# A second cross attention rebuilt as a stream of seven stages, with row turns, router logits and routing inside it

## The reference

```
x += tanh(g_xattn[0]) * cross_attention_0(layernorm(x), ctx)      # 16 heads of 64
x += tanh(g_ffn[0])   * six layers of (local attention, ffn)(layernorm(x))
x += tanh(g_xattn[1]) * cross_attention_1(ctx, layernorm(x))      # this change
x += tanh(g_ffn[1])   * mixture_of_experts(layernorm(x))          # and its router
```

```
attn  = softmax(q k^T / sqrt(8))                 # keys, values from ctx; 64 x 64 per head
gate  = 0.5 * mean_n(ctx @ w_la) + 0.5 * max_n(ctx @ w_la)        # one number per head
attn2 = softmax(gate * attn)
out   = (w * attn2 + (1 - w) * attn) @ v @ w_proj + b_proj
```

## Time and profile before

| | us |
|---|---|
| median of 3 runs (4242.39 to 4248.78) | 4245.28 |
| the profiled execution | 4245.7 |
| its span, first to last instruction | 4243.9 |

### The profile page before, as it was taken

How to read it: one execution, slowest core, us unless ns; L and a number is a source line. 1 busy time by engine, 2 the same in 40 slices (tenths; PEclk the granted TensorE clock), 3 DMA queues, 4 the chain that set the end, 5 groups by cost and what they waited for, 6 DMA issues and landing times.

```text
span 4243.9 us, 147344 instructions
## 1 busy us (share of the span) xinstructions
PE 4020.4 (95%) x50345; PEld 2806.3 (66%) x50345; DVE 3504.6 (83%) x7236; ACT 2999.4 (71%) x6796; POOL 2867.3 (68%) x3647
## 2 busy tenths in 40 slices
PE   5999998999999999999999999999999998788799
PEld 3777775666666666666666666666666666566665
DVE  4666667999888998899988998899989998677566
ACT  2555556888888888788878887888888887554322
POOL 2333337888888888888887888788888887555200
PEclk9999999999999999999999999999999999887699
DMA  3000001000000001000000001000010000000000
GB/s 89 6 7 7 6 4 48 10 8 10 24 22 9 9 8 34 12 8 9 24 21 8 10 7 31 16 10 7 10 35 11 7 10 9 18 12 11 2 10 10
DMA packets 162227, 64.81 MB, mean 15 GB/s; under 512 B 121556, under 2 KB 156128, under 8 KB 162016
## 3 DMA queue, kind: packets, MB, share of 16 engines
q1 hardware_dynamic: 162016, 62.05, 5.8%
HBM read 26.54 MB, written 2.10 MB: 7 GB/s over the span
## 4 chain that ended last, share of the span: by engine, by line
POOL 43%; issue 25%; PE 24%; DVE 5%; POOLq 2%; SPq 1%; ACT 1%; DVEq 0%; DMA 0%; ACTq 0%
POOL qn L646 10%; POOL qn L635 8%; POOL big L646 7%; POOL e L641 5%; POOL big L635 4%; PE pj L1506 3%; PE pp L1464 2%; PE po L1479 2%; PE sc L1861 2%; PE pj L1498 2%; PE pj L1547 1%; POOL rstd L657 1%; PE po L1485 1%; POOLq L389 1%; PE turn L1450 1%
## 5 line engine op out<-in xcount | busy, mean ns | idle before, releaser
L1573 PE MATMUL pj<-wqkv,xcT 128*128 128x512 f32 x1536 | 799.5, 602 | 17.0 <-issue 9.2
L646 POOL TENSOR_TENSOR qn<-qn,big 128x512 f32<-128x512 f32 x384 | 490.5, 1278 | 289.9 <-DVE big L1139 289.9
L818 ACT ACTIVATE big<-pj 128x512 f32<-128x512 f32 x768 | 473.7, 617 | 69.0 <-PE pj L1573 59.2
L1139 DVE TENSOR_TENSOR big<-pj,ropes 128x512 f32<-128x512 f32 x768 | 521.3, 679 | 0.0
L1145 DVE TENSOR_REDUCE ss<-big 128x8 f32<-128x512 f32 x768 | 514.8, 671 | 0.1
L646 POOL TENSOR_TENSOR big<-big 128x512 f32<-128x512 f32 x384 | 485.1, 1273 | 4.7 <-DVE big L1139 4.7
L1726 PEld LDWEIGHTS pp<-wo,oT 128*128 128x128 f32 x3072 | 358.7, 192 | 161.7 <-issue 82.6
L641 POOL TENSOR_TENSOR e<-e,rc 128x512 f32<-128x512 f32 x384 | 400.2, 1042 | 55.7 <-DVE rc L1169 55.7
L635 POOL TENSOR_TENSOR qn<-qn,ny 128x512 f32<-128x512 f32 x384 | 396.7, 1043 | 7.5
L635 POOL TENSOR_TENSOR big<-big,ny 128x512 f32<-128x512 f32 x384 | 396.2, 1043 | 7.6
L1726 PE MATMUL pp<-wo,oT 128*128 128x128 f32 x3072 | 395.4, 282 | 2.3 <-ACT oT L841 1.2
(11 more groups left out here) (320 smaller groups left out, 9938.3 us busy)
## 6 DMA issues: line engine op xcount, KB each, us to landing
wqkv<-in_L_ffn_Wqkv SPq DMA_DIRECT2D x18, 512.0 KB, 3.7
xsd<-Y SPq DMA_DIRECT2D x192, 32.0 KB
xsd<-Y SPq DMA_DIRECT2D x384, 15.8 KB
xsf<-Y SPq DMA_DIRECT2D x96, 64.0 KB
xsf<-Y SPq DMA_DIRECT2D x192, 31.5 KB
xsx<-Y SPq DMA_DIRECT2D x64, 64.0 KB, 1.8
xsx<-CT SPq DMA_DIRECT2D x64, 64.0 KB, 1.9
wo<-in_L_ffn_Wo SPq DMA_DIRECT2D x6, 512.0 KB, 4.2
```

Of the source, the lines that this page charges most:

```text
L646: nc.gpsimd.tensor_tensor(U[a.par][i], U[a.par][i], t2b[i % 2], ALU.add).then_inc(sem("d_add"), 1)
L818: nc.scalar.activation(sqb[i % 2], pj[i % 2][:, :], ACT.Square).then_inc(sem("d_sq"), 1)
L1139: nc.vector.tensor_tensor(t2v, swapped, sin, ALU.mult).then_inc(sem("d_r"), 1)
L1573: mm(pj[i % 2][:, :], xcT[:, a.par, :], wqkv[:, i * 512:i * 512 + 512], start=True, stop=True).then_inc(sem("d_ch"), 1)
```

## The change

The stream gets seven stages, called p[0] to p[6], and each body becomes a list of small functions called in a new order. Work is the same but for what follows.

- **Stages**: the row turn is a step of its own ahead of the projections. The second softmax and its turn share stage p[3], the first softmax with its values is in p[2]. p[6] is a tile whose residual was done two steps earlier.
- **Banks**: the row turn goes to pj[0], where the projections follow it. Turned probabilities of the first softmax go to pt_, of the second to pp (the other way round before). The gates go to columns of po[0], beside the value products, instead of pj[1]. The router's logits lie there too, and turned rows in po[1].
- **Scores** are done in two halves at two places: scores(p1, 0) late in one step, scores(p2, 1) first in the next.
- **Row turns and logits inside**: values2 also turns a normalised row tile, ACT copies it to CT (in the loop also to tmp, where PE reads it), and values1 multiplies it with the router weights. Normalised rows go to two small buffers r_in, not to Y. Tiles 30 and 31 are turned after the stream, and tiles 28 to 31 get their logits there.
- **DVE** loses two small instructions per tile (L1302 and L1330): a scalar_tensor_tensor takes the constant with it.
- **Routing** for tiles 0 to 27 is put behind DVE's steps 34, 35 and 36 (7, 8 and 4 instructions, with an exponential on ACT). That of tiles 28 to 31 (19 small instructions) lies ahead of and between the first group's experts.
- **Experts**: the first group is written out, the other seven are the loop. PE issues up of the first expert right behind the last residual, ahead of the last row turns.

The core of the diff (conditions on missing tiles, and functions whose instruction is unchanged, are cut):

```diff
-        r_turn = [pt_, pp, pj[0], pj[1]]
-        r_logits = po[0][:, 0:NT * NE].rearrange("p (t x) -> p t x", x=NE)
+        l_gates, r_logits = po[0][:, 144:144 + L1H], po[0][:, 160:160 + NT * NE].rearrange("p (t x) -> p t x", x=NE)
+        r_rows = po[1][:, 144:144 + 2 * P]
+        r_in = [xsd[:, i, :] for i in range(2)]
+        FIRST = NT - MT
...
@@ POOL
+                second_logits(p[3], 0)
+                second_logits(p[3], 1)
+                gate_rows(p[2])
+                out_sum(p[4])
+                key_rows_masked(p[1], 0)
+                key_rows_masked(p[1], 1)
+                gate_halves(p[1])
+                variance(p[4])
+                bias_row(p[0])
+                inverse_deviation(p[4])
+                gate_sum(p[1])
...
@@ ACT
+                tile_turned(p[1])
+                exp1(p[2], 1)
+                turned1(p[2], 0)
+                row_turned(p[4], p[6])
+                keys_queries(p[1])
+                out_turned(p[4])
+                exp2(p[3], 0)
+                turned1(p[2], 1)
+                turned2(p[3], 0)
+                exp2(p[3], 1)
+                values(p[1])
+                turned2(p[3], 1)
+                if p[3] and isinstance(p[3].g, int) and p[3].g == NT - 1:
+                    act.wait_ge(sem("r_st"), 2)
+                    nc.scalar.activation(r_buf[0][:, 0:FIRST, :], r_buf[0][:, 0:FIRST, :], ACT.Exp).then_inc(sem("r_e"), 1)
+                exp1(p[1], 0)
...
@@ DVE
+                def weighted(k, i, rc, dst, done):
+                    nc.vector.scalar_tensor_tensor(l_heads(dst), l_out[k][:, :, 0:16].rearrange("p k (a d) -> p k a d", a=2), law[:, i:i + 1],
+                                                   bc(l_pairs(rc), L1D), ALU.mult, ALU.mult).then_inc(sem(done), 1)
...
+                normalise(p[6])
+                inverse1(p[3])
+                max1(p[2], 0)
+                second_scale(p[3])
+                sub1(p[2], 0)
+                max1(p[2], 1)
+                sub1(p[2], 1)
+                inverse2(p[4])
+                weighted2(p[4])
+                max2(p[3], 0)
+                sub2(p[3], 0)
+                weighted1(p[3])
+                max2(p[3], 1)
+                gate_stats(p[1])
+                sub2(p[3], 1)
+                residual(p[4])
+                stats(p[4])
+                aggregate(p[4])
+                for stage, (first, n) in ROUTED.items():
+                    if p[stage] and isinstance(p[stage].g, int) and p[stage].g == NT - 1:
+                        route(first, n)
...
+            ROUTED = {3: (0, 7), 4: (7, 15), 5: (15, ROUTE_STEPS)}
...
+                    if known:
+                        route_rest(2 + 2 * ex, 4 + 2 * ex)
...
@@ PE
+                scores(p[2], 1)
+                values2(p[4], p[6])
+                turn1(p[2], 0)
+                project(p[1])
+                out_turn(p[4])
+                turn1(p[2], 1)
+                out_project(p[4])
+                turn2(p[3], 0)
+                values1(p[2], p[6])
+                scores(p[1], 0)
+                turn2(p[3], 1)
+                tile_turn(p[0])
...
             past(pe, "l_res", NT)
+            past(pe, "r_c", NT - 2)
+            up(0, True, 0)
+            past(pe, "l_y", NT)
+            for i in range(2):
+                last = nc.tensor.transpose(r_rows[:, i * P:i * P + P], r_in[i], ident)
+            last.then_inc(sem("r_T"), 1)
+            past(pe, "r_c", NT)
+            for t in range(FIRST, NT):
+                last = route_logits(t, CT[:, t, :])
+            last.then_inc(sem("r_lg"), 1)
```

More of the change, by code:

```diff
@@ L967, in l_body, with turned1 @@
[L967 to L973 removed]
+                def turned1(tile, h):
+                    if tile:
+                        past(act, "l_T1", tile.g * 2 + (h + 1))
+                        past(act, "l_P1", tile.g)
+                        nc.scalar.copy(l_pT[0][h], pt_[:, :]).then_inc(sem("l_C1"), 1)
@@ new lines, in scores, with four, turn1 @@
+                        last.then_inc(sem("l_s"), 1)
+                def four(bank, src):
+                    for j in range(4):
+                        last = nc.tensor.transpose(bank[:, j * P:j * P + P], src[:, j * P:j * P + P], ident)
+                    return last
+                def turn1(tile, h):
+                    if tile:
+                        past(pe, "l_ex1", tile.g * 2 + (h + 1))
+                        past(pe, "l_C1", tile.g * 2 + h)
+                        four(pt_, l_e1[tile.par % 2][h]).then_inc(sem("l_T1"), 1)
@@ new lines, in turn2, with pv @@
+                def turn2(tile, h):
+                    if tile:
+                        past(pe, "l_ex2", tile.g * 2 + (h + 1))
+                        past(pe, "l_C2", tile.g * 2 + h)
+                        four(pp, l_e2[tile.par % 2][h]).then_inc(sem("l_T2"), 1)
+                def pv(tile, k):
+                    for q8 in range(8):
+                        for bb in range(BT):
+                            q = slice(bb * 64, bb * 64 + 64)
+                            last = mm(l_out[k][q, q8, :], l_pT[k][q8 // 4][:, (q8 % 4) * P + bb * 64:(q8 % 4) * P + bb * 64 + 64],
+                                      l_vp[tile.par][:, bb, q8, :], start=True, stop=True)
+                    last.then_inc(sem("l_P%d" % (k + 1)), 1)
@@ new lines, in up, with down @@
+            def up(m, known, ex):
+                pe.wait_ge(sem("m_hT"), m * NEX + max(ex - 1, 0))
+                rows = (CT[:, 0:MT, :] if known else CT[:, bass.ds(m * MT, MT), :]).rearrange("p a t -> p (a t)")
+                mm(h_banks[ex % 2][0][:, :], expert_T(1, ex), rows, start=True, stop=True)
+                mm(h_banks[ex % 2][1][:, :], expert_T(3, ex), rows, start=True, stop=True).then_inc(sem("m_h"), 1)
+            def down(m, ex):
+                pe.wait_ge(sem("m_hT"), m * NEX + (ex + 1))
+                pe.wait_ge(sem("m_acc"), m * NEX + (ex - 1 if ex >= 2 else 0))
+                for j in range(MT):
+                    last = mm(sc[:, (ex % 2) * 512 + j * P:(ex % 2) * 512 + j * P + P], pT[:, ex % 2, j * P:j * P + P], expert_T(2, ex), start=True, stop=True)
+                last.then_inc(sem("m_y"), 1)
```

626 lines of the change are left out of this document (314 added, 312 removed).

## The result

The changed kernel takes 4230.8 us (median of 8 runs, 4226.67 to 4244.71), the kernel before, measured beside it, 4251.88: ratio 0.9957, 95% interval 0.9943 to 0.9971. The forecast was 4170 with a range of 4145 to 4207, so the time lies outside it. The profiled execution is 4226.67 us with a span of 4224.8, against 4245.7 and 4243.9.

A forecast was written before the change was run, and what follows sets the result against it. The prediction saw a stream bound by a chain of waits across engines, then a serial row, logit and routing piece. Its terms, -1 + 55 + 3.5 + 17.5 = 75 us gained, gave 4170 from 4245.7, range 4145 to 4207.

The forecast's parts named there:

- The first factor: Start of the second cross attention's stream: before at 3643.2, put at 3644, a loss of 1 us.
- The full-clock beat: Time per tile in the stream at 2.4 GHz: a loop through DVE, ACT and PE summing to 8.5, taken as 8.6 us.
- PE's floor of 8.2: PE's own work in one stream step at full clock, summed to 8.2 us, the least a step could take.
- The scores in halves: Splitting the scores over two places in a stream step: extra PE time between nothing and 1.09, taken as 0.9 us.
- The clock: In the new stream the lower clock level would hold 10% of the time, making the beat 9.0 us.
- the prediction's own formula: Stream beat as full-clock step over (1 - lower-level share x 0.45): 8.6 / (1 - 0.1 x 0.45) = 9.0 us.
- From the last factor to the last residual: End of the stream: 18.1 us before, forecast 14.0 plus 0.5 for hand-overs, gain 3.5.
- The tail: From the last residual to the first expert's way down: 30.5 us before, 13.0 forecast, gain 17.5.
- The clock keeps falling: Rival, 20 in 100: the stream keeps the old 31% share of the lower clock, beat 10.0, time 4201.
- The new order only moves the wait: Rival, 9 in 100: an unfound queue wait keeps the stream's old beat of 10.78, time 4225.
- PE closes its gaps: Rival, 10 in 100: the stream's beat is PE's floor, 8.2, at full clock, time 4145.
- The slower case: Rival, 3 in 100: the clock stays low for most of the stream, where PE's step is 15.7 against 13.6.

The follow-up runs named there:

- dense_in_loop: Changed kernel plus one unread 384-column matmul per tile between the scores and the second half's turn, where PE does not wait: 4223.4 us, ratio to before 0.9935.
- dense_after: Changed kernel plus one unread 384-column matmul per tile ahead of the output projection: 4196.6 us, ratio to the kernel before 0.9868.
- thin_after: Changed kernel plus sixteen unread 18-column matmuls per tile ahead of the output projection: 4205.7 us, ratio to the kernel before 0.9906.
- together_rows_out: Changed kernel with both score halves in one place and row turns, logits and routing after the stream: 4183.8 us, ratio to the kernel before 0.9851.
- scores_together: Changed kernel with both halves of the scores back in one place, late in the step: 4192.1 us, ratio to the kernel before 0.9852.
- logits_early: Changed kernel with the row's logit matmul moved ahead of PE's wait for ACT's last copy: 4191.1 us, ratio to the kernel before 0.9865.

## Why the prediction was wrong, point by point

**The first factor** was forecast at 3644 and came at 3644.65. Right.

**The full-clock beat** is the step that failed first: "I take 8.6 at the full clock". It was the right loop, but every term of it was too short, 8.51 in all for 9.49. 0.48 of the 0.98 stands between ACT's last copy and the scores. I had put logits, gates and products at 1.45, they take 1.68; and the hand-over to PE at 0.05, it takes 0.30. That this loop sets the step is shown: 0.75 us of PE work inside it (dense_in_loop) lengthen the step by 0.69, the same work in PE's wait (dense_after) by 0.05, and taking the logits ahead of the wait shortens it by 0.2. The joined scores, which spare PE 1.0 us, shorten it by only 0.4, and the rows' removal by 0.5, so another limit stands close behind; which one was not followed. PE's floor of 8.2 was too low as well. In thin_after PE hardly waits: its step of 9.94, less the 1.04 of the added matmuls and some 0.14 of a wait ahead of them (0.63 from start to start for a group of four turns that takes 0.49 elsewhere), leaves 8.8 for PE's own work. So with the scores in halves and the rows inside, 8.6 was below what PE alone needs. Among what was missing are the row's turn (0.26 between starts for 0.11), the halves of the scores (2.0 for 1.92), the value products (2.08 for 2.0) and the tile's turn (0.31 for 0.22). At 31 steps 9.49 in place of 8.6 costs 28 us. The engines' own sums were short too, outside the loop: in a step DVE has 7.71 for 7.2 and POOL 6.77 for 6.2; ACT's 6.00 for 6.1 was right.

**The scores in halves.** I took 0.9 for a half. It is 1.00 to the next start (3793.24 to 3794.24), and the whole, all eight rows, takes 1.02 (3795.51 to 3796.53). So halving saves nothing: doing the halves in two places costs PE a full microsecond a step more. The Trainium skill (TensorE: Matmul & The Clock Gate, Part 3: Packing small matmuls) says that a pack lasts about one matmul; the trace agrees. Against my 0.9 that is 0.10 a step, 3 us over the stream, where I had put the rule's price at 6.

**The clock.** "I put the lower level at 10% of the time" was wrong: 0.85 over the stream is 30%. With 9.49 and 30% the prediction's own formula gives 9.49 / (1 - 0.30 x 0.45) = 11.0, and 10.74 was measured. A step wholly at the lower level didn't occur. By the same formula the steps of 13.52 at 0.67 and 14.55 at 0.62, of which 67% and 77% were at the lower level, come to 17.2 and 17.4 for one wholly there; this is an estimate, and 15.7 was forecast. It is 1.8 times the full-clock step, as the forecast had it, so a microsecond at the lower level cost what was assumed; the share and the full-clock step did not fit. I had argued from gaps of 5%; the records show 2% and the clock fell just the same. Of the miss in the beat, 1.74 x 31 = 54 us, 26 are this. The two failures hang together. Among the kernels with all of the change's work, and nothing added, the clock over the stream is 0.85 at a full-clock step of 9.5, 0.94 at 9.3, 0.93 at 9.1 and 0.99 at 8.9: whatever shortened the step also raised the clock, though not in strict order. The length of the step can't be the cause by itself, since dense_after has 0.99 at 9.5 and thin_after at 9.9. What the clock would be at a step of 8.6 with all of the change's work, no run shows; together_rows_out, without the rows, has 0.99 (2% at the lower level) at 8.76 over all.

**From the last factor to the last residual** 14.0 were added up, with 0.5 for hand-overs; it took 17.5. The timeline of the changed kernel:

```profile
3977.88 2.05 POOL L749 TENSOR_TENSOR qn<-e,l_c 128x512 f32<-128x512 f32 x2
...
3978.87 1.11 PE L1907 MATMUL po<-big 128*64 128x18 f32 x32
3980.03 0.26 DVE L1383 RECIPROCAL l_r<-po 128x16 f32<-128x16 f32 x1 [2.23 <-PE po L1907]
3980.32 0.35 DVE L1359 SCALAR_TENSOR_TENSOR oT<-po,law,l_r 128x128 f32<-128x128 f32 x1
3980.59 0.68 DVE L1372 TENSOR_REDUCE mx<-qn 128x8 f32<-128x512 f32 x1
...
3982.89 0.69 DVE L1378 TENSOR_TENSOR qn<-qn,mx 128x512 f32<-128x512 f32 x1
...
3983.87 0.59 ACT L1010 COPY big<-pp 128x512 f32<-128x512 f32 x1 [1.21 <-PE pp L1888]
...
3984.35 0.63 ACT L1004 ACTIVATE qn<-qn 128x512 f32<-128x512 f32 x1
...
3986.67 0.39 ACT L1042 ACTIVATE kbuf<-kbuf 128x224 f32<-128x224 f32 x1
...
3989.11 0.34 DVE L1413 TENSOR_SCALAR xsd<-X,dif,rstd 128x128 f32<-128x128 f32 x1
...
3989.70 0.45 PE L1935 MATMUL po<-K,xsd 128*128 128x128 f32 x1 [3.55 <-DVE xsd L1413]
```

From the factor to the end of the second logits' subtraction (3983.58) it is 5.95 for 3.7. It was not POOL: the first of its two multiplications was done after half of the 2.05. DVE's queue has inverse2 (L1383) and its weighting (L1359) ahead of max2 (L1372), and inverse2 waits for PE's products of the tile before, which end at 3979.98: DVE stands idle for 2.23, and max2 starts 2.96 after the factor. The prediction's sum has no such wait. Another 0.8 went on ACT: the second half's exponential starts at 3984.35, not at 3983.58, since the copy of the first half's turn stands ahead of it. The rest is as described: five routing instructions and the normalise stand ahead of values2, which waits for them.

**The tail** was forecast at 13.0 and took 13.4. Its order is as the prediction has it (statistics, twelve routing instructions, two turns, four logits, table load, way down). No cost of the other small routing instructions shows: from the way down to the end of the span it is 1.6 us shorter than before.

**The rivals.** "The clock keeps falling" described the share (30% for its 31%), with a time of 4201, since it kept the beat of 8.6. "The new order only moves the wait" has the time, 4225, but not by its cause: POOL's wait ahead of the output sum fell from 2.39 to 0.83 in a full-clock step, and what holds the beat is a longer loop together with the clock. "PE closes its gaps" came true in the records only. The slower case was not far off: the stream gained 1.2 us in all.

The terms against the profiled execution: forecast 4245.7 - 75 = 4170.7, measured 4226.7, a miss of 56.0. 54 are the beat, 3.0 the end of the stream, 0.65 the first factor, 0.4 the tail, and 1.6 came back in the experts: 56.4.

**Open.** What in TensorE's work the clock's fall goes by was not found. Neither the busy share of the records (0.98 at 0.85; 0.88 in together_rows_out, at 0.99) nor the width of the matmuls nor the waits alone orders the runs. Each clock figure of the stream is that of one profiled run, but the mean clock over the whole execution, which every timed run has, goes the same way: 0.977 to 0.981 in the changed kernel, 0.985 to 0.989 in scores_together, 0.988 to 0.993 in dense_after, 0.986 to 0.988 in logits_early, 0.973 to 0.979 in the kernel before.

## What to carry to other kernels

Before a dependent loop is put at so much, add for each change of engine the time that the trace shows at such a place, and count every small matmul by its distance to the next start: six terms, each 0.06 to 0.48 us short, were 30 us over 31 steps. Put small work ahead of a wait and not behind it, and leave matmuls together that already run side by side. Where PE's records fill a stretch and its clock still falls, compare start distances with those of a kernel that has more work there: what looks busy may be a wait.

## What the runs showed of the hardware that was not expected

- Useless matmuls made a kernel faster. 384 columns a tile, 0.75 us of PE time, raised the granted clock from 0.85 to 0.99 and took some 38 us off by the ratios; 16 matmuls of 18 columns did the same to the clock and took some 22 off. The Trainium skill (TensorE: Matmul & The Clock Gate, A second HAM failure mode) puts such falls, in a kernel of its own, down to idle moments between groups of matmuls; that agrees with the waits which the starts show, but not with together_rows_out, whose records leave PE idle for 12% of the stream at a clock of 0.99.
- Half of a packed group lasts as long as the group: the four rows of half the scores last 1.08 us, the eight rows of the whole 1.09.
- One matmul between ACT's copy and the gates, 0.3 us of a 9.5 us step, decided some 40 us of 4230, most of it by way of the clock.
